# One-hots of 320 keys of every third pair moved from ScalarE to VectorE, in a message-passing kernel on one core

## The reference, cut to what matters

```python
x_j = x[src]
v_j = x_j[:, :384].reshape(E, 128, 3)
s_j = silu(x_j[:, 384:] @ W1 + b1) @ W3 + b3
rbf = jnp.sqrt(2.0 / R_CUT) * jnp.sin(n * jnp.pi * r / R_CUT) / r
edge_basis = rbf * cutoff @ W2 + b2
s1, s2, s3 = split(s_j * edge_basis)                 # 128 columns each
v_msg = v_j * s1[:, :, None] + s3[:, :, None] * edge_attr1[:, None, :]
x = x + jax.ops.segment_sum(concat([v_msg, s2]), dst, num_segments=N_NODES)
...
x_j = x[src]                                         # depends on the sender only
msg = concat([v * s1, dot + s3])                     # of U, V, Wu1, Wu2
x = x + jax.ops.segment_sum(msg, dst, num_segments=N_NODES)
```

## Time and profile before

| | us |
|---|---|
| timed executions, median of 3 | 641.67 |
| lowest, highest | 639.85, 643.99 |
| span of the profiled execution, first to last instruction | 638.7 |
| median of the timed ones less that span | 3.0 |
| PE busy | 538.3 (84%) |
| DVE busy | 471.8 (74%) |
| ACT busy | 446.0 (70%) |
| POOL busy | 367.8 (58%) |

### The profile page before, as it was taken

The page is one execution under the profiler, slowest core; times in us unless marked ns, Lnnn a source line. Parts: engine busy times, 40 slices in busy tenths (PEclk is TensorE's granted clock), DMA queues, the critical chain, the costliest instruction groups (busy, mean ns, idle before and its releaser), DMA issues.

```text
span 638.7 us, 14716 instructions
## 1 busy us (share of the span) xinstructions
PE 538.3 (84%) x5281; PEld 298.4 (47%) x5281; DVE 471.8 (74%) x796; ACT 446.0 (70%) x835; POOL 367.8 (58%) x405
## 2 busy tenths in 40 slices
PE   5647598888988998889978998888998899699996
PEld 3313244444544553555544554554554455355442
DVE  3886577788878877888787887978887768553385
ACT  3333476677877895888797788778797779659300
POOL 8827666666656666666666666766665563532300
PEclk9755797989989999999999999989998899999998
DMA  8837777777777777778777777778777775040122
GB/s 241 302 125 233 223 214 213 225 236 221 215 207 231 218 220 238 218 213 239 214 224 234 226 214 238 209 223 243 215 217 210 226 217 157 18 128 33 36 84 83
DMA packets 48067, 125.83 MB, mean 197 GB/s; under 512 B 9539, under 2 KB 22409, under 8 KB 47985
## 3 DMA queue, kind: packets, MB, share of 16 engines
q0 software_dynamic: 25120, 102.91, 55.0%
q1 hardware_dynamic: 18433, 15.76, 8.0%
q10 hardware_dynamic: 4432, 6.10, 3.0%
HBM read 112.73 MB, written 12.00 MB: 195 GB/s over the span
## 4 chain that ended last, share of the span: by engine, by line
PE 56%; ACT 19%; issue 13%; DVE 4%; another core or an unknown queue 4%; DMA 2%; POOL 1%; SPq 0%; ACTq 0%; DVEq 0%; POOLq 0%
PE psum L1382 11%; PE psum L1487 10%; PE psum L1376 7%; ACT side L708 7%; PE psum L1344 6%; PE psum L1356 6%; ACT scratch L717 6%; PE psum L1337 4%; PE psum L1390 3%; PE psum L1402 2%; PE psum L1366 2%; DMA work<-in_edge_attr 2%; ACT total L722 1%; PE psum L1420 1%
## 5 line engine op out<-in xcount | busy, mean ns | idle before, releaser
L584 POOL DMA_INDIRECT side<-node_table,src_c x234 | 232.6, 994 | 130.5 <-remote 69.5
L708 ACT ACTIVATE side<-key_no,less_key 128x320 bf16<-128x320 f32 x314 | 160.1, 564 | 0.3
L1376 PE MATMUL psum<-side,scratch 128*32 128x512 f32 x468 | 129.7, 631 | 9.0 <-ACT stage L728 7.0
L1382 PE MATMUL psum<-side,scratch 128*32 128x128 f32 x1404 | 126.6, 285 | 10.7 <-issue 10.2
L717 ACT ACTIVATE scratch<-side,one_f 128x640 bf16<-128x640 bf16 x157 | 129.0, 822 | 0.0
L1071 DVE TENSOR_TENSOR side<-side,psum 128x512 f32<-128x512 f32 x117 | 79.9, 683 | 46.2 <-PE psum L1344 23.5
L584 POOL DMA_INDIRECT work<-node_table,src_c x80 | 80.7, 1008 | 57.4 <-remote 26.7
L1074 DVE TENSOR_TENSOR side<-side,psum 128x768 f32<-128x768 f32 x117 | 110.9, 948 | 0.0
L663 ACT CAST scratch<-psum 128x512 bf16<-128x512 f32 x79 | 46.2, 584 | 82.9 <-remote 51.1
L1382 PEld LDWEIGHTS psum<-side,scratch 128*32 128x32 f32 x1404 | 77.9, 112 | 37.1 <-issue 35.0
L1344 PE MATMUL psum<-w2s,scratch 128*128 128x384 bf16 x314 | 81.1, 341 | 2.4 <-issue 2.3
(11 more groups left out here) (226 smaller groups left out, 776.1 us busy)
## 6 DMA issues: line engine op xcount, KB each, us to landing
side<-node_table,src_c POOLq DMA_INDIRECT x234
sum_rows<-stage SPq DMA_DIRECT2D x208, 16.0 KB
sum_rows<-zeros_bf SPq DMA_DIRECT2D x1, 2688.0 KB, 20.7
node_table<-work ACTq DMA_DIRECT2D x8, 320.0 KB, 3.6
scratch<-sum_rows SPq DMA_DIRECT2D x10, 256.0 KB
work<-sum_rows SPq DMA_DIRECT2D x10, 256.0 KB, 2.7
out<-xw SPq DMA_DIRECT2D x9, 256.0 KB
xw<-in_x ACTq DMA_DIRECT2D x1, 1728.0 KB
```

What stands on the lines that cost most here:

```text
L584: g.indirect_dma_start(out=rows[i % SLOT_PAIRS][:, j, :], out_offset=None, in_=node_table, in_offset=bass.IndirectOffsetOnAxis(ap=src_c[:, ...
L708: a.activation(key_off[:, b, j, :], key_no[:, :], ACT.Abs, bias=less_key[:, t:t + 1]).then_inc(L["key_off_made"], 1)
L1376: mm(bank[b][j * SPAN:(j + 1) * SPAN, :], hot[:, n % 2, t + j, 0, :], rows[s][:, j, 0:4 * C], start=first, stop=True, skip_group_check=True)
L1382: last = mm(bank[b][(2 + j) * SPAN:(3 + j) * SPAN, k * C:(k + 1) * C], hot[:, n % 2, t + j, 1 + k, :], rows[s][:, j, 4 * C:5 * C], start=f ...
```

## The change

VectorE now makes the key one-hots of the third pair of every group (i = 3n+2), and ACT those of the other two. A new step `key_equals(n)` stands on DVE right behind the products of pair 3n, ahead of any step of a piece there. For each of the two tiles it is one instruction with two operations: `key_no_short + less_key`, then compare with 0. Its keys are a 16-bit copy of `key_no`. Before writing, it waits for `counted` of group n-2, since the one-hots have two buffers by group. ACT skips `key_offsets` and `key_hots` for these pairs, and PE's `count` waits for the new semaphore before its last four tiles. Other functions only count their semaphores anew.

```diff
+        key_no_short = sb("key_no_short", [P, KEYS], U16)
...
+        def by_compare(pair):
+            return pair % GP == GP - 1
+        def by_distance(pairs):
+            return sum(1 for i in range(pairs) if not by_compare(i))
...
+            then(g.tensor_copy(key_no_short[:, :], key_no_i))
...
             def key_offsets(i):
-                b = i % 2
-                if i >= 2:
-                    act.wait_ge(L["key_hot_made"], i - 1)
+                done = by_distance(i)
+                b = done % 2
+                if done >= 2:
+                    act.wait_ge(L["key_hot_made"], done - 1)
...
                 for i in range(PAIRS + 1):
-                    if i < PAIRS:
+                    if i < PAIRS and not by_compare(i):
                         key_offsets(i)
-                    if i:
+                    if i and not by_compare(i - 1):
                         key_hots(i - 1)
...
+            def key_equals(n):
+                t = 2 * (GP - 1)
+                if n >= 2:
+                    dve.wait_ge(L["counted"], n - 1)
+                for j in range(2):
+                    k = GROUP * n + t + j
+                    last = v.tensor_scalar(key_hot[:, n % 2, t + j, :], key_no_short[:, :], less_key[:, k:k + 1], 0.0,
+                                           ALU.add, ALU.is_equal)
+                last.then_inc(L["key_equal_made"], 1)
...
                 for i in range(PAIRS):
                     messages(i, rows_in)
                     n = i // GP
+                    if i % GP == 0 and n < LG:
+                        key_equals(n)
                     if i % GP == 1 and n >= 2:
                         add_counts(n - 2)
...
-                pe.wait_ge(L["key_hot_made"], GP * n + tiles.stop // 2)
+                pe.wait_ge(L["key_hot_made"], by_distance(GP * n + tiles.stop // 2))
+                if tiles.stop >= GROUP:
+                    pe.wait_ge(L["key_equal_made"], n + 1)
```

More of the change, by code:

```diff
@@ L265, in build @@
         sums_back = [sem(f"sums_back{b}") for b in range(SUM_BUFS)]
-        loop_names = """products_made basis_made src_hot_made key_off_made key_hot_made hot_made counted summed
+        loop_names = """products_made basis_made src_hot_made key_off_made key_hot_made key_equal_made hot_made counted summed
         copied combined sums_taken counts_taken table_step stored start_in angle_made turn_near turn_made sin_made wave_made
@@ L438, in _ @@
                     sp.wait_ge(L["src_hot_made"], LG)
-                    sp.wait_ge(L["key_off_made"], 2 * PAIRS)
-                    sp.wait_ge(L["key_hot_made"], PAIRS)
+                    sp.wait_ge(L["key_off_made"], 2 * by_distance(PAIRS))
+                    sp.wait_ge(L["key_hot_made"], by_distance(PAIRS))
+                    sp.wait_ge(L["key_equal_made"], LG)
                     sp.wait_ge(L["hot_made"], 2 * LG)
@@ L711, in key_hots @@
             def key_hots(i):
-                n, b = group_of(i), i % 2
+                n, done = group_of(i), by_distance(i)
+                b = done % 2
                 t = 2 * (i - GP * n)
-                act.wait_ge(L["key_off_made"], 2 * i + 2)
+                act.wait_ge(L["key_off_made"], 2 * done + 2)
                 if n >= 2:
@@ L1231, in _ @@
                 with dve.Fori(0, EXTRA) as r:
-                    dve.wait_ge(L["key_off_made"], 2 * PAIRS)
+                    dve.wait_ge(L["key_off_made"], 2 * by_distance(PAIRS))
                     dve.wait_ge(L["sums_taken"], LG)
```

## The result

| | before | after |
|---|---|---|
| median of 19 runs each | 641.23 | 648.92 |
| lowest to highest | 635.83 to 644.23 | 643.02 to 655.34 |
| ratio, 95% interval | | 1.012 [1.010, 1.0139] |
| span of the profiled execution | 638.7 | 646.9 |

The changed kernel is slower by 7.7 us, 1.2%, where 36 us were forecast. The page of the changed kernel: busy time, granted clock, and the chain by engine and by line.

The account below looks back on a forecast made before the run. PE and POOL were taken to set the loop's step together, 9.34 us a group. A new circle of 10.05 adds 0.71 us times 51, 36 us: 638.7 + 36 = 675, with 3.0 more 678; range 650 to 720.

Parts of the forecast that it names:

- circle: Once a group, DVE's wait for counts of n-2, compares, products, PE and hand-over: 10.05 us against 9.34, 36 us in all.
- term for PE: PE from the start of turn 3n+1 to the end of the counts: 6.33 us in one group, 6.1 taken as mean.
- rival A: In the loop the old step holds, PE's delay hidden while its signals lie unseen: 639 to 646, say 642; chance 0.16.
- compares, piece step, products: DVE's leg at pair 3n: compares 0.5, piece step 0.7 on the mean, products with semaphores 1.75 us.
- hand-over to DVE: From the end of PE's counts until DVE sees them: 0.14 to 2.1 us, 1.0 taken.
- Compares: Two new DVE compares a group: 0.24 to 1.09 us, 0.5 taken, 26 us of bare work over the loop.
- ScalarE: ACT loses a third of its one-hot work in 52 groups: 101 us less, worth 0, 28 us at the far end.
- B (gathers): Compares meet the first gather of a pair and delay POOL's step by 0.3 us a group: 657; chance 0.20.
- C (ACT the bound): L708 and L717 hold 83 us of the chain; a third less makes the kernel faster, 614; chance 0.12.
- Promised signs: In the loop: DVE idle over 2 us a group before compares, PE about 82% busy, group step near 10, ACT about 345.

Follow-up runs that it names:

- late: Kind of chip where engines often go on 1 to 2 us after PE finishes what they wait for; before 641.23, changed 648.92.
- second late pair: The unaltered changed kernel timed again beside the kernel before (650.93) on another chip with late signals: 657.98, ratio 1.0101.
- prompt chip: Kind of chip where engines mostly go on within 0.1 us of PE; the changed kernel there against 556.30: 572.29, ratio 1.0299.
- plain copies: SyncE's copies of the same 256 rows replace POOL's two gathers a pair; late chip: kernel before 542.18, changed 569.13; prompt chip: kernel before 539.43.
- relief alone: Changed kernel without compares and their waits, ScalarE making third-pair one-hots only in the first two groups; against kernel before 556.90: 557.62, ratio 1.0025.
- compares alone: Kernel before plus two compares a group to an unread spare tile, no wait on counted, ScalarE's work unchanged: 564.96, ratio 1.0158 against 556.90.
- moved compares: Changed kernel with compares moved behind the sender one-hots of pair 3n+1, where no wait is added; against kernel before 556.90: 559.24, ratio 1.0046.

## Why the prediction was right or wrong

**The circle exists; its term for PE was too long.** The kernel did come out over 1% slower, as forecast, but 7.7 us in place of 36 and not by the forecast's path: in the first pair of traces the middle of the loop did not get longer. So the direction is owed in good part to luck. Measured at 648.9, it lies just under the forecast's own range from 650 and inside the whole one only because that took in rival A. The circle's legs can be read from the trace of the changed kernel, as the mean over groups 9 to 49: from the first compare to the end of the products of 3n+1, to PE's basis turn, to the end of the counts, to the next first compare.

| leg | forecast | after (late) | second late pair | prompt chip |
|---|---|---|---|---|
| compares, piece step, products | 2.95 | 2.97 | 2.95 | 3.00 |
| PE, turn 3n+1 to end of counts | 6.1 | 5.37 | 5.45 | 5.05 |
| hand-over to DVE | 1.0 | 1.07 | 1.21 | 0.20 |
| sum | 10.05 | 9.41 | 9.61 | 8.25 |

(The 0.1 us from products to PE's turn is in the first leg.) The circle closes: the sum is, to 0.05, the step of the changed kernel over the same groups, 9.36, 9.57 and 8.25. The step of the prediction that failed is "PE from the start of turn 3n+1, 460.94, to the end of the counts, 467.27: 6.33; I take 6.1 for the mean". As a mean of the kernel before that is near, even a little short: over the same 41 groups it is 6.39, from 4.79 to 9.74. But it is not a fixed cost that can be carried over into the circle. With 5.37 in its place the sum is 9.32 against the old 9.34, and the forecast 642, rival A's time.

In the kernel before the products of 3n+1 were ready 2.12 us before PE's turn, and PE then took 6.39. In the changed one the slack is 0.10 and PE takes 5.37. PE's rows show where this time was, over all three turns of a group. Before, 90 to 512 us:

```profile
L1376 PE MATMUL psum<-side,scratch 128*32 128x512 f32 x404 | 111.4, 631 | 8.7 <-ACT stage L728 7.0 <-issue 1.6
L1382 PE MATMUL psum<-side,scratch 128*32 128x128 f32 x1212 | 108.2, 284 | 5.2 <-issue 4.7
L1344 PE MATMUL psum<-w2s,scratch 128*128 128x384 bf16 x268 | 68.2, 337 | 1.0 <-issue 0.8
L1356 PE MATMUL psum<-scratch 128*128 128x320 bf16 x268 | 59.7, 328 | 6.6 <-issue 6.5
...
L1390 PE MATMUL psum<-total,stack 128*32 128x128 f32 x358 | 32.4, 280 | 8.9 <-issue 8.7
L1337 PE MATMUL psum<-ident_bf,scratch 128*64 128x128 bf16 x536 | 30.1, 228 | 14.6 <-issue 13.1 <-ACT work L761 1.0 <-ACT side L755 0.4
```

After, 94 to 516 us:

```profile
L1403 PE MATMUL psum<-side,scratch 128*32 128x512 f32 x408 | 113.5, 636 | 0.3 <-ACT stage L741 0.3
L1409 PE MATMUL psum<-side,scratch 128*32 128x128 f32 x1218 | 93.3, 286 | 0.0
L1369 PE MATMUL psum<-w2s,scratch 128*128 128x384 bf16 x272 | 69.3, 337 | 60.6 <-issue 25.2 <-DVE side L1097 23.5 <-DVE work L1097 5.6
L1383 PE MATMUL psum<-scratch 128*128 128x320 bf16 x272 | 58.9, 325 | 1.0 <-issue 1.0
...
L1417 PE MATMUL psum<-total,stack 128*32 128x128 f32 x360 | 31.0, 302 | 0.9 <-issue 0.9
...
L1362 PE MATMUL psum<-ident_bf,scratch 128*64 128x128 bf16 x544 | 29.2, 228 | 7.4 <-issue 2.8 <-ACT work L760 2.2 <-ACT side L761 1.5
```

Five of the six rows had 44.0 us of idle time inside PE's turns (8.7 + 5.2 + 6.6 + 8.9 + 14.6) and have 9.6 now. The small sums (L1382, now L1409) cover 15 us less for the same matmuls of the same length: they stood apart before and run closer together now. Now PE waits ahead of its turns, 60.6 us before the basis or 1.3 a group. Pauses at the head of a turn stand where there were pauses inside it, most of them "issue".

Why the pauses inside went is open. It may be the later start, or ScalarE's sooner copies (of the 7.0 us after L728 0.3 are left in the row). The plain copies narrow it down. On the late chip, with ScalarE's work as before and the products ready 0.71 us ahead of PE's turn, the kernel before takes 4.98 for this leg, where with gathers it takes 6.34. The versions with gathers on prompt chips have 4.96 to 5.12, among them the relief alone with 4.96 and, with ScalarE's work as before, the compares alone with 4.97. So the pauses come with the gathers on a late chip and are no part of PE's own work. The small sums over the whole run, with gathers on the first late chip and with plain copies (L1392) on the second:

```profile
L1382 PE MATMUL psum<-side,scratch 128*32 128x128 f32 x1404 | 126.6, 285 | 10.7 <-issue 10.2
```
```profile
L1392 PE MATMUL psum<-side,scratch 128*32 128x128 f32 x1404 | 98.4, 275 | 0.0
```

On a prompt chip the relief alone gained nothing; on a late one it wasn't timed.

**The hand-over, and what POOL has to do with it.** The changed kernel at 329 us, a late hand-over (start, duration, instruction, idle before):

```profile
329.63 0.95 POOL L595 DMA_INDIRECT side<-node_table,src_c  x1 [0.30 <-issue]
329.87 0.33 PE L1383 MATMUL psum<-scratch 128*128 128x320 bf16 x1
331.34 0.58 ACT L674 CAST scratch<-psum 128x512 bf16<-128x512 f32 x1 [1.73 <-remote]
331.61 0.51 DVE L1082 TENSOR_SCALAR scratch<-key_no_short,less_key 128x320 bf16<-128x320 uint16 x2 [1.17 <-PE psum L1383]
331.78 0.94 POOL L595 DMA_INDIRECT side<-node_table,src_c  x1 [1.21 <-remote]
331.82 0.27 ACT L741 COPY stage<-psum 128x128 f32<-128x128 f32 x1
```

The counts end at 330.20 inside a gather that lasts to 330.58. DVE, ACT and POOL all go on between 331.34 and 331.82, DVE 1.41 us after the counts. The same kernel on a prompt chip:

```profile
301.42 0.76 PE L1383 MATMUL psum<-scratch 128*128 128x320 bf16 x4
...
301.66 0.95 POOL L595 DMA_INDIRECT side<-node_table,src_c  x1 [0.30 <-issue]
...
302.23 0.65 DVE L1082 TENSOR_SCALAR scratch<-key_no_short,less_key 128x320 bf16<-128x320 uint16 x2 [1.48 <-PE psum L1383]
```

The counts end at 302.18 inside a gather too, and DVE starts 0.05 us later. The 1.0 us that was forecast for the hand-over measured 1.07, and 1.21 in the second late trace. Those are means of very different values, from 0.04 to 2.16.

**Compares.** Forecast 0.5 us for two, measured 2 x 0.307 = 0.61 by the group's row. By the Trainium skill ("VectorE: DVE Perf Modes", Side-by-side) the estimate was 240 ns for one; the trace has 307, so here that estimate is 67 ns short. Which part of it is off, no run shows.

**ScalarE.** Forecast: 101 us of work gone, worth 0. The worth was right as far as it was timed (1.0025 with the relief alone, on a prompt chip). The lengths of all ACT's instructions add up to 100.5 us less, as forecast, but its busy time fell from 446.0 to 362.4, 84 us: instructions in a row overlap, and busy time counts an overlap once. 160.1 us for 314 of L708 is 0.51 for each, not the mean of 0.564 that I multiplied. So the forecast's ACT of 345 us was too low.

**Rivals.** A (old step holds) is what the middle of the loop did, but not for the reason given alone: PE's turns were shorter by 1.0 us a group. Whether some of the delay also lay hidden in the hand-over, as A has it, is not settled: before, the add waited in 31 of the 41 groups and came 1.68 us after the counts' end there, and now the compares come 1.07 after it over all 41. B (gathers) falls: 989 ns after against 994, and the change costs more with the gathers gone. 40 gathers of the changed kernel start inside a compare, the one at 331.78 above among them; they took 0.95 us on the mean, no more than the usual length. The slow gather of the earlier trace rows is no rule for every VectorE operation. C (ACT the bound) falls: ACT's share of the chain fell from 19% to 4% and the time rose.

**The 7.7 us.** A's 642 lacks them. In the second pair of traces on a late chip (spans 646.5 and 653.5) the difference is 1.5 before the first product, 0.1 to pair 9, 3.2 in the middle and 2.2 from pair 144 on; in the first pair it was 2.3, 2.8, -1.1 and 4.1. Ahead of the first product none of the compares runs, only POOL's small copy of the key numbers is new. And one and the same kernel (the moved compares) has that start at 53.6 and at 56.3 in two traces from one prompt chip, so this part can't be charged to the change. The end is slower in both. The last gathers are over by 540 us. Before, 530 to 548, and after, 538 to 556:

```profile
530.00:548.00 18.00, 16.83 (x212) 9.98 (x202) 15.69 (x26) 17.71 (x35) 5.49 (x5) 1.00 0.35 102
```
```profile
538.00:556.00 18.00, 13.60 (x139) 7.80 (x141) 15.25 (x26) 10.22 (x22) 1.60 (x1) 0.81 0.11 36
```

PE is busy 13.60 us of 18 where it was busy 16.83, and its granted clock fell to 0.81, that is to the lower level for part of the stretch, where it had been 1.00. On the second late chip the last groups have 0.96 after and 1.00 before. The rest of the 7.7 us is spread, and no run isolates it.

**Promised signs.** Seen: idle time moved from the add to the compares; products behind the compares; PE's share of the window 88% to 82% (363.22 / 445); compares of 0.3 each; a granted clock of 0.96 in the window where it was 0.97. Not seen: a group step near 10 (9.36) and over 2 us of idle time a group before the compares (1.5).

## What to carry to other kernels

When a new wait closes a circle between engines, time each leg as it will run once the engine enters it late, not as it runs today: a leg that contains pauses may give some of its length back, and here 1.0 of 6.4 us decided between +36 and about 0. Removing 98 us of work from ScalarE, which is busy for 81% of the window before the change, was worth nothing where it was timed alone, while some 31 us of compares, with their wait, cost 27.0 once VectorE was 98% busy and no gathers hid them. Put such work where its wait has been made anyway: the same compares one pair later cost 3.1 us instead of 16.0 on a prompt chip. And time a change on more than one chip before believing its size.

## What the runs showed of the hardware

The same kernel takes 641 to 651 us in two sets of timings and 556 to 557 in four, on three other chips. Idle time of POOL before its gathers, on a late chip 132.8 us with 58.7 of it put down to remote (above); the same kernel and row on a prompt chip:

```profile
L595 POOL DMA_INDIRECT side<-node_table,src_c x234 | 239.6, 1024 | 72.7 <-issue 67.0 <-PE psum L1409 5.7
...
L1082 DVE TENSOR_SCALAR scratch<-key_no_short,less_key 128x320 bf16<-128x320 uint16 x104 | 28.5, 317 | 11.9 <-PE psum L1383 11.4
```

A gather is no faster on a prompt chip (1024 ns against 989); what goes is the waiting for signals, 76.8 to 11.9 us before the compares. With plain copies in place of the gathers both kinds take 539 to 542 us. So a change can cost 1.2% on one chip and 3.0% on the next with no other difference in the code. Why the chips differ stays open.
